# Flamingo gated layer on one core: the routed sums are added into the rows by the DMA that loads them, and not by VectorE

## The reference

```python
x = x + tanh(g_xattn[0]) * xattn(layernorm(x), ctx, mask, Wq, Wk, Wv, Wo)     # 16 heads of 128, 361 context tokens
x = x + tanh(g_ffn[0]) * ffn(layernorm(x), ...)

def ffn(x, ...):
    x = x + causal_self_attention(rms(x, w_ln1)) @ wo                          # 16 heads of 32, rope
    h = rms(x, w_ln2).reshape(B * S, H)
    probs = softmax(h @ w_router)                                              # 8 experts
    combine = one-hot of the top 2, times their probability
    y = einsum('eti,eih->eth', silu(g) * u, w_down_e)                          # g, u: h through w_gate_e, w_up_e, 352 wide
    routed = einsum('eth,te->th', y, combine)
    sh = silu(h @ w_sh_gate) * (h @ w_sh_up) @ w_sh_down                       # 1408 wide
    sh = sh * sigmoid(h @ w_sh_eg)
    return x + (routed + sh).reshape(B, S, H)
```

## Time and profile before

| | us |
|---|---|
| median of three runs | 926.47 |
| the runs | 923.95 to 930.01 |
| the profiled execution, its own time | 930.65 |
| its span, first to last instruction | 928.9 |
| TensorE busy | 899.1 (97%) |
| VectorE busy | 646.2 (70%) |
| ScalarE busy | 560.9 (60%) |
| GpSimd busy | 322.0 (35%) |

### The profile page before, as it was taken

How to read it: one execution, slowest core, us unless ns; L and a number is a source line. 1 busy time by engine, 2 the same in 40 slices (tenths; PEclk the granted TensorE clock), 3 DMA queues, 4 the chain that set the end, 5 groups by cost and what they waited for, 6 DMA issues and landing times.

```text
span 928.9 us, 16126 instructions
## 1 busy us (share of the span) xinstructions
PE 899.1 (97%) x5713; PEld 837.1 (90%) x5713; DVE 646.2 (70%) x1482; ACT 560.9 (60%) x1448; POOL 322.0 (35%) x344
## 2 busy tenths in 40 slices
PE   8989999999999999999999999899999999999996
PEld 7989999999999999999987878799999999999996
DVE  3547777774446778784286985848585988897863
ACT  3656667664555666674433766745436787877851
POOL 3432222335552223234653542335400133323221
PEclk8989999999999999999999999999999999999999
DMA  5732730005550000002542121124338999999975
GB/s 155 221 93 79 220 94 1 1 12 169 153 163 24 17 1 1 1 12 66 149 124 78 58 59 47 51 57 124 112 101 285 300 322 312 317 304 329 310 191 153
DMA packets 112760, 122.20 MB, mean 132 GB/s; under 512 B 9887, under 2 KB 77927, under 8 KB 112680
## 3 DMA queue, kind: packets, MB, share of 16 engines
q1 hardware_dynamic: 97806, 98.80, 34.2%
q0 software_dynamic: 5184, 12.13, 5.9%
q10 hardware_dynamic: 9690, 10.24, 3.9%
HBM read 110.72 MB, written 19.07 MB: 140 GB/s over the span
## 4 chain that ended last, share of the span: by engine, by line
PE 65%; DVE 16%; DMA 9%; ACT 4%; issue 4%; POOL 1%; ACTq 0%; SPq 0%; DVEq 0%
PE bank L2078 59%; DMA eraw<-in_L_ffn_w_gate_e_dram 6%; PE bank L2225 4%; DVE we L1356 2%; DVE wf L1356 1%; ACT we L928 1%; DVE sm L1587 1%; DMA sums<-s_sum 1%; DMA raw<-s_unit 1%; DMA raw<-in_L_xattn_Wq_dram 1%; DMA X<-in_x_dram 1%; DVE TE L1786 1%; DVE PQ L1563 1%; DVE stat L1623 1%; DVE PQ L1561 1%
## 5 line engine op out<-in xcount | busy, mean ns | idle before, releaser
L1947 POOL TENSOR_SCALAR SC<-SC,mx,anyv 100x361 f32<-100x361 f32 x128 | 82.0, 651 | 205.3 <-DVE mx L1463 191.9
L1356 DVE TENSOR_TENSOR we<-eraw,we 128x704 fp32r<-128x704 f32 (+2 forms) x140 | 107.3, 802 | 24.7 <-ACT we L928 24.4
L928 ACT ACTIVATE we<-eraw 128x704 fp32r<-128x704 f32 (+2 forms) x140 | 96.7, 718 | 37.6 <-DMA eraw<-in_L_ffn_w_gate_e_dram 21.5
L1930 POOL TENSOR_TENSOR wx<-raw,wx 128x512 fp32r<-128x512 f32 x64 | 83.3, 1310 | 76.6 <-ACT wx L914 76.3
L1930 POOL TENSOR_TENSOR wf<-raw,wf 128x512 fp32r<-128x512 f32 x54 | 71.6, 1333 | 103.6 <-ACT wf L914 103.5
L2078 PE MATMUL bank<-H2h,wf 128*128 128x400 f32 x352 | 100.2, 351 | 0.0
L1045 ACT ACTIVATE SC<-SC,mx 100x361 f32<-100x361 f32 x128 | 75.4, 594 | 19.9 <-DVE mx L1476 19.5
L2078 PE MATMUL bank<-XTh,wx 128*128 128x400 f32 x256 | 71.6, 353 | 0.7 <-POOL wx L1930 0.7
L2078 PE MATMUL bank<-QOh,wx 128*128 128x400 f32 x256 | 70.9, 348 | 1.0 <-DVE mx L1476 1.0
L2008 POOL DMA_INDIRECT XB<-s_h,inv x20 | 21.9, 1094 | 143.4 <-PE bank L2524 113.3
L914 ACT ACTIVATE wf<-raw 128x512 fp32r<-128x512 f32 x100 | 61.6, 628 | 15.0 <-DMA raw<-s_unit 7.2
(11 more groups left out here) (289 smaller groups left out, 2672.3 us busy)
## 6 DMA issues: line engine op xcount, KB each, us to landing
raw<-s_unit SPq DMA_DIRECT2D x60, 256.0 KB, 3.6
eraw<-in_L_ffn_w_gate_e_dram SPq DMA_DIRECT2D x40, 352.0 KB, 4.6
eraw<-in_L_ffn_w_up_e_dram SPq DMA_DIRECT2D x40, 352.0 KB, 5.2
eraw<-in_L_ffn_w_down_e_dram SPq DMA_DIRECT2D x40, 256.0 KB, 5.4
raw<-in_L_xattn_Wq_dram SPq DMA_DIRECT2D x32, 256.0 KB, 2.9
raw<-in_L_xattn_Wo_dram SPq DMA_DIRECT2D x32, 256.0 KB, 2.8
eraw<-in_L_ffn_w_down_e_dram SPq DMA_DIRECT2D x20, 192.0 KB, 5.2
s_unit<-in_L_ffn_w_sh_gate_dram SPq DMA_DIRECT2D x11, 256.0 KB, 3.7
```

The lines of the kernel that those rows point to most:

```text
L928: eng.activation(weights("e", u)[0:rows, 0, 0:n], eraw[u % 6][0:rows, 0:n], ACT.Copy).then_inc(sem("act_e"), 1)
L1356: return eng.tensor_tensor(o, src, f32(hi), ALU.subtract)
L1930: eng.tensor_tensor(w[:, 1, :, :], raw[plan.raw[stream, u] % 4][:, :, :], f32(w[:, 0, :, :]), ALU.subtract).then_inc(sem("pool_w"), 1)
L1947: eng.tensor_scalar(sc, sc, m[:, 3, h:h + 1], anyv[:, b:b + 1], ALU.mult, ALU.mult).then_inc(sem("pool_p"), 1)
```

## The change

The four loads of `load_sums` get an adding operation and write into `Z` itself. The buffer `sums` and VectorE's eight `final` steps are gone. GpSimd's loads now wait, beside the last scatter, for the scaling of Z (`dve_zf`) and, for batches 0 to 3, for the first half's shared rows (`dve_sr`). VectorE's shared rows of the second half wait for the load of their own two batches (`dma_sum2`, `dma_sum3`) in place of all eight additions, and the stores of batches 0 to 3 wait for `dma_sum0` and `dma_sum1`.

```diff
--- before.py
+++ after.py
@@ -320,9 +320,6 @@
     s1 += [take(last, 2), take(last, 2)] + last
     yield from steps_routed(s1)
     yield ("sums",)
-    yield from take(s1, len(s1) - 3)
-    for b in range(B):
-        yield ("final", b)
     yield from take(s1)
     for i in range(HB):
         yield ("srow", 1, i)
@@ -690,7 +687,6 @@
     TE = A2.ring("TE", 2, [128, 3 * 128])
     ATh = A2.ring("ATh", 2, [128, 3, 128], R)
     ATl = A2.ring("ATl", 2, [128, 3, 128], R)
-    sums = Region(nc, half1, after1).place("sums", [T, B, D])
     s_h2 = nc.dram_tensor("s_h2", (HROWS, D), F, kind="Internal").ap()
     s_sum = nc.dram_tensor("s_sum", (TROWS, D), F, kind="Internal").ap()
 
@@ -831,7 +827,7 @@
 
         def store(b):
             if b < HB:
-                sp.wait_ge(sem("dve_fin"), b + 1)
+                sp.wait_ge(sem(f"dma_sum{b // 2}"), 16)
             else:
                 sp.wait_ge(sem("dve_sr"), b + 1)
             eng.dma_start(out[b], Z[:, b, :]).then_inc(sem("dma_out"), 16)
@@ -1798,16 +1794,9 @@
             dve.wait_ge(sem("dve_zf"), B)
             dve.wait_ge(sem("dve_route"), ROUTE["sg", h])
             if h:
-                dve.wait_ge(sem("dve_fin"), B)
+                dve.wait_ge(sem(f"dma_sum{b // 2}"), 16)
             bank = banks[plan.bank["srow", h, i]]
             stt(Z[:, b, :], bank[0:T, :], sg[:, b:b + 1], Z[:, b, :], ALU.mult, ALU.add).then_inc(sem("dve_sr"), 1)
-
-        def final(b):
-            dve.wait_ge(sem(f"dma_sum{b // 2}"), 16)
-            dve.wait_ge(sem("dve_zf"), B)
-            if b < HB:
-                dve.wait_ge(sem("dve_sr"), b + 1)
-            eng.tensor_tensor(Z[:, b, :], Z[:, b, :], sums[:, b, :], ALU.add).then_inc(sem("dve_fin"), 1)
 
         for name, *a in steps_head():
             if name == "x_stat":
@@ -1911,8 +1900,6 @@
                 scale(*a)
             elif name == "srow":
                 shared_row(*a)
-            elif name == "final":
-                final(*a)
 
 
     def pool_program(eng):
@@ -2020,9 +2007,12 @@
 
         def load_sums():
             pool.wait_ge(sem("dma_add"), 16 * NB)
+            pool.wait_ge(sem("dve_zf"), B)
             for k in range(B // 2):
+                if 2 * k < HB:
+                    pool.wait_ge(sem("dve_sr"), 2 * k + 2)
                 src = s_sum[k * 2 * T:(k + 1) * 2 * T, :].rearrange("(b t) d -> t b d", t=T)
-                eng.dma_start(sums[:, 2 * k:2 * k + 2, :], src).then_inc(sem(f"dma_sum{k}"), 16)
+                eng.dma_start(Z[:, 2 * k:2 * k + 2, :], src, accum_op=ALU.add).then_inc(sem(f"dma_sum{k}"), 16)
 
         eng.memset(Z[:, HB:B, :], 0.0).then_inc(sem("pool_const"), 1)
         eng.memset(eps1[:, :], 1e-5).then_inc(sem("pool_const"), 1)
```

## The result

The changed kernel takes 932.16 us (median of nine runs, 930.12 to 936.74) against 926.47 (nine runs, 923.95 to 932.52). The ratio of the times is 1.0069, with a 95% interval of 1.0050 to 1.0088: slower by 4.6 to 8.2 us, and within the 1% named beforehand. The single profiles say less than the ratio does. The span after is 928.3 us and before 928.9, because in this execution the work ahead of the tail was some 5 us quicker (the last scatter is issued at 899.19 instead of 904.24; the mean granted clock was 0.995 against 0.987, and nothing there was changed). So I read the tail: from the issue of the first load to the end of the span it was 928.9 - 909.34 = 19.56 us before and is 928.3 - 904.27 = **24.03 us** now, +4.5 us.

A forecast was written before the change was run, and what follows sets the result against it. The tail was bound by two side-by-side paths, the sums' and TensorE's. Adding makes the loads 3.8 us dearer; two rows and 4.25 us follow the last, giving +0.7: 926.47 + 0.7 = 927.2 us, range 922.5 to 934.5.

The forecast's parts named there:

- the likeliest case: Tail: adding loads run at 160 GB/s, span +0.7 us, median 927.2; chance 0.68 together with D.
- Where the change acts: Chain's end, where TensorE runs out of work; the 65% of the chain on TensorE is untouched.
- The bound of the gain, 1.75 us: VectorE's tail: without the eight additions the end comes at most 1.75 us earlier, since TensorE's transposes set it.
- The price of adding, 10.2 us of all engines at 160 GB/s: Four loads: 10.2 us of all DMA engines against 6.4 plain, from the queue rows' average over twenty scatters.
- the two bounds: Cost of the four loads: 6.4 us as plain loads, 14.1 us at the lone last scatter's 116 GB/s.
- Load 3 at 10.9 + 3.8 = 14.7 us after the first issue: Last of the four loads: lands 3.8 us later than the plain one, at about 924.0 instead of 920.2.
- rival C: Adding loads run on 10 of 16 engines: +6.9 us at 100 GB/s (near end), +13.2 at 72.5; chance 0.14.
- Stores in the way, up to 2.1 us: Shared DMA engines in the tail: stores of batches 0 to 3 could delay the last load by 2.1 us.
- The two rows behind load 3, and the end 4.25 us behind VectorE: After the last load: two shared rows of 0.68 us, then 4.25 us to the span's end, some tenths less.
- GpSimd's waits, the buffer: GpSimd's new waits are met over 80 us before the loads; the buffer given up costs and brings nothing.
- Rival B: Adding in the loads costs nothing extra: -1.75 us, median 924.7; chance 0.18.
- D: Last load lands between 920 and 923.3: gain from 1.75 us to none; chance 0.68 together with the likeliest case.

The follow-up runs named there:

- e2: Changed kernel with plain loads into the buffer sums and nothing added (routed sums left out of the result): 926.64 us, ratio to before 0.9988.
- e5: Changed kernel with each adding load issued only after the one before it has landed, all stores after the last load: 948.36 us (one run).
- e3: Changed kernel with all stores held until the last adding load has landed: 936.48 us, ratio to before 1.0112.
- e10: As e3, but adding loads of rows 0 to 95 of each batch alone, the rest left out: 927.46 us (one run).
- e7: As e5, but adding loads of rows 0 to 95 of each batch alone, the rest left out: 940.58 us (one run).
- e8: Changed kernel with one adding load of rows 96 to 99 of all eight batches, then four of rows 0 to 95: 933.33 us, ratio to before 1.0054.
- e9: As e2, but the plain loads cut into eight of one batch each, nothing added: 925.07 us (one run).
- e12: Kernel before, its eight additions kept on VectorE, with the loads cut into eight plain ones of one batch each: 926.15 us, ratio to before 1.0010.

## Why the prediction came out as it did

The forecast was 927.2 us, within 1%, in 922.5 to 934.5; measured 932.16, within 1%. The sign of the likeliest case was right, its size was not: +0.7 us forecast, +5.7 between the medians. That the time still lies in the range owes something to luck: +5.7 is above what the likeliest case gave without the stores (+4.6 at 116 GB/s), and the range was as wide as it was because it took in C's near end and the stores' full delay, of which the runs show no clear sign for load 3.

- *Where the change acts.* Right. The instructions ahead of the last scatter are the same, TensorE's end is where it was, and the whole loss fits in the tail.
- *The bound of the gain, 1.75 us.* Right: e2 has 1.56 us. The six additions on the path were worth that and not 4.1 us, because TensorE's transposes stand behind them.
- *The price of adding, 10.2 us of all engines at 160 GB/s.* Near: 11.6 us in after, 11.2 in e5, 10.1 for 96 rows at 156 GB/s. The term between the two bounds was the right one to take; the queue rows told more than the lone scatter.
- *Load 3 at 10.9 + 3.8 = 14.7 us after the first issue.* **This is the step that failed.** It turned engine time into landing time as if the loads stayed spread over all 16 engines. Measured: 19.0 us, 20.6, and 19.2 with no store beside. The term missing is what 100 rows cost against 96, 7 us between e3 and e10, most of it, by the estimate above, engines that stand idle. It was the mechanism of rival C ("the accumulating loads run on fewer engines"), whose near end was +6.9 us and which got 0.14. C's evidence, the stores' 0.62, was the right row. What was wrong in C is that the four don't stay on the same 10 engines: together they reach 0.88 to 1.06 and only then fall to 0.42. The Trainium skill ("DMA: Bandwidth & Descriptors", "Why a DMA increments its semaphore by 16 and not by 1") has 10 engines for 100 rows and 16 for 96, with an exception for some direct copies. For lone adding loads e5 against e7 agrees with it (a share of 0.67 and 7.1 us, up to 1.14 and 5.0 us); the four loads of e8, of 96 rows too, should by it have had all engines, and their landings, the first after 11.6 us, don't show it.
- *Stores in the way, up to 2.1 us.* Not shown as a cost to load 3: it lands at 19.2 us without them, 19.0 and 20.6 with them.
- *The two rows behind load 3, and the end 4.25 us behind VectorE.* 1.5 us and 3.55, so "some tenths off" was 0.7.
- *GpSimd's waits, the buffer.* As said, at nothing. Not foreseen: GpSimd needs 5.47 us to issue the four loads and not 3.33, and the first data comes about 2.1 us after the first issue, where before it took 1.6.
- *Rival B* is refuted by 19.0 us against 10.9; *D* as well.

What stays open: which engines serve which load, since the profile doesn't name them. Each engine that serves three of the four loads would have three times 4.0 us of work and end some 15 us after the first issue, and 19.2 were measured. And why e8 lost what e10 gained.

## What to carry to other kernels

An addition on an engine is worth only what lies between it and the next thing that is late: here eight additions of 0.685 us were worth 1.6 us, and moving them into the DMA cost 6 to 7.6. Before costing a transfer by its bytes, ask over how many engines its rows divide, and look for a share of the DMA engines that stays flat below 1: 96 rows landed 7 us earlier than 100. But measure the cut before you count on it: with the last four rows in a load of their own (e8) nothing of the 7 us was left. A transfer at the end of a program is paid by its landing, not by its mean engine time.

## What the hardware showed unexpectedly

- An adding DMA into SBUF runs at about 156 GB/s when it has all 16 engines (1.57 MB in 10.1 us), where the plain loads take 5.3 to 6.8 us of all engines for 1.64 MB. Its packets of 2 KB take 178 ns at the median (e3, e10), a plain store's 93 on average (after).
- A lone adding load of 100 x 2 rows of 2 KB takes 7.1 us, of 96 x 2 rows 5.0 us.
- GpSimd needs 1.30 to 1.45 us to issue an adding load of 400 KB when alone, 0.78 to 0.91 for a plain one, 0.56 to 0.65 for a plain one of one batch.
- The same 1.64 MB of plain loads as eight single batches cost 5.3 us of all engines and as four pairs 6.7 to 6.8, with the last landing at 9.8 to 10.1 instead of 10.9 to 11.1 us (e9 and e12 against before and e2).
